# Attention added into x by accumulating transfers, h's low products apart, x's maximum one step ahead

## The reference, cut to what matters

```python
# x: 64 x 128 x 256 (batch, sequence, model); ctx the same shape
q, k, v = (LN(x) @ Wq + bq), (ctx @ Wq + bq), (ctx @ Wq + bq)      # 16 columns
corr = mean over batch and columns of circular correlation(q, k)    # 128 values
w, shift = softmax(top_k(corr, 12)), indices
R = sum_i w[i] * roll(v, -shift[i])          # repeated for 16 heads, reshaped
x = x + R @ Wout + bout
def q4(x):   # blocks of 16: scale = max|x| / 6, values to a grid of 8 with signs
    ...
n = layernorm(x)
h = silu(q4(n) @ q4(w_gate).T) * (q4(n) @ q4(w_up).T)               # 704 columns
x = x + q4(h) @ q4(w_down).T
```

## Time and profile before

| | |
|---|---|
| median of 3 runs | 575.65 us |
| the profiled execution | 575.05 us, span 573.2 us |
| VectorE busy | 461.9 us (81%) |
| TensorE busy | 466.7 us (81%) |
| ScalarE busy | 393.3 us (69%) |
| GpSimd busy | 282.7 us (49%) |
| DMA engines busy, first 50 us / main loop | 82% / 57% |
| main loop, one step | 12.9 us |

### The profile page before, as it was taken

One profiled execution on the slowest core, in us unless ns is written; L12 is line 12 of the kernel. 1 busy time (PEld: TensorE's weight loads), 2 busy tenths in 40 slices (PEclk: granted clock), 3 DMA queues, 4 the chain that ended last, 5 costly groups with the idle time before them and its releaser, 6 DMA issues. The chain is left out here.

```text
span 573.2 us, 10039 instructions
## 1 busy us (share of the span) xinstructions
PE 466.7 (81%) x3454; PEld 306.1 (53%) x3454; DVE 461.9 (81%) x742; ACT 393.3 (69%) x666; POOL 282.7 (49%) x365
## 2 busy tenths in 40 slices
PE   5086798704789999999899999999899999999944
PEld 5075687501345565556555555556555565556633
DVE  2899864315799999999899999999899999998760
ACT  2177865535778777788888777788888778776530
POOL 3045351035356666656556666656556666632221
PEclk9689999775989999999999999999999999999987
DMA  9956550043145556555655557645655556544533
GB/s 283 344 170 202 176 186 14 25 102 75 37 97 122 110 122 127 120 106 111 128 118 119 110 123 126 121 107 110 130 116 119 112 115 110 108 88 98 88 78 78
DMA packets 165042, 69.19 MB, mean 121 GB/s; under 512 B 129152, under 2 KB 164736, under 8 KB 164992
## 3 DMA queue, kind: packets, MB, share of 16 engines
q1 hardware_dynamic: 164416, 68.03, 52.2%
q10 hardware_dynamic: 576, 0.53, 0.3%
HBM read 27.90 MB, written 9.18 MB: 65 GB/s over the span
## 5 line engine op out<-in xcount | busy, mean ns | idle before, releaser
L694 PE MATMUL ps<-guT_hi,a_xT 128*128 128x512 f16 (+1 forms) x384 | 140.7, 366 | 55.2 <-DMA a_xT<-ctx_sb 55.2
L405 POOL TENSOR_TENSOR ctx_sb<-h_c,sl 128x704 f16<-128x704 f16 x64 | 96.1, 1523 | 115.8 <-DVE ctx_sb L909 115.8
L704 PE MATMUL ps<-dT_hi,hqT 128*128 128x256 f16 x704 | 132.2, 276 | 12.3 <-DMA hqT<-ctx_sb 12.3
L696 PE MATMUL ps<-guT_hi,a_xT 128*128 128x512 f16 (+1 forms) x384 | 140.3, 365 | 0.0
L695 PE MATMUL ps<-guT_lo,a_xT 128*128 128x512 f16 (+1 forms) x384 | 140.1, 365 | 0.0
L694 PEld LDWEIGHTS ps<-guT_hi,a_xT 128*128 128x128 f16 x384 | 37.7, 98 | 103.7 <-DMA a_xT<-ctx_sb 46.0
L457 ACT ACTIVATE h_c<-y_h 128x1408 bf16<-128x1408 bf16 (+3 forms) x40 | 49.2, 1230 | 61.9 <-DVE y_h L939 36.5
L706 PE MATMUL ps<-dT_lo,hqT 128*128 128x256 f16 x384 | 89.6, 277 | 0.0
L704 PEld LDWEIGHTS ps<-dT_hi,hqT 128*128 128x128 f16 x704 | 69.7, 99 | 25.2 <-DMA hqT<-ctx_sb 13.1
L443 POOL TENSOR_TENSOR xs<-xs,w_raw 128x512 f32<-128x512 f32 x32 | 37.8, 1180 | 79.5 <-issue 49.6
L904 DVE SCALAR_TENSOR_TENSOR hb<-ps,h_in,w_raw 128x704 f32<-128x704 f32 x64 | 60.5, 945 | 4.7 <-PE ps L696 4.6
(11 more groups left out here) (139 smaller groups left out, 868.8 us busy)
## 6 DMA issues: line engine op xcount, KB each, us to landing
w_raw<-a_scratch SPq DMA_DIRECT2D x64, 128.5 KB, 2.6
xs<-in_x_dram SPq DMA_DIRECT2D x16, 512.0 KB, 5.3
ctx_sb<-in_ctx_dram SPq DMA_DIRECT2D x16, 512.0 KB, 4.4
out_dram<-a_xT SPq DMA_DIRECT2D x64, 128.0 KB, 2.0
hqT<-ctx_sb SPq DMA_TRANSPOSE x64, 3.7
w_raw<-in_L_ffn_w_down_dram SPq DMA_DIRECT2D x1, 704.0 KB, 8.1
w_raw<-in_L_ffn_w_gate_dram SPq DMA_DIRECT2D x1, 640.0 KB, 5.9
w_raw<-in_L_ffn_w_up_dram SPq DMA_DIRECT2D x1, 640.0 KB, 7.1
```

What stands on the lines that cost most here:

```text
L405: pool.tensor_tensor(hq[:, j % 2, t, FF:2 * FF].rearrange("p (ih r) -> p ih r", ih=IH), h_c[:, :].bitcast(F16).rearrange("p (ih t r) -> p ...
L694: pe.matmul(dst, xt[:, c, :], guT[0][:, c, n0:n1], start=(c == 0), stop=False)
L696: last = pe.matmul(dst, xt[:, KC + c, :], guT[0][:, c, n0:n1], start=False, stop=(c == KC - 1))
L704: pe.matmul(dst, hqT[:, j % 4, c, :], dT_hi[:, c, :], start=(c == 0), stop=False)
```

## The change

The attention goes from HBM straight into x: GpSimd issues transfers that add what they bring to what is there. `xs` gets a 257th column for the mean, so one transfer adds both. `a_scratch` is laid out so that each of 8 rows holds all batch elements side by side, and one transfer takes two pairs (the first two take one each): 17 transfers, issued at the end of every second step, for pairs st + 6 and st + 7. Lines 443 and 444 and SP's loads go.

The statistics, normalisation and maximum of x each run one pair further ahead, with two buffers for `xn`; the loop starts at step -4. The maximum (949 in the changed file) stands behind y_x.

`low_h` handles one tile. The first stands where it stood; the second at the end of the step, behind a wait for y_x, and SP's second `turn_h` stands behind `turn_x`. `h_c` gets a second buffer. The factor on the scales moves into other constants, which makes the copy `s32` (428) superfluous.

```diff
-FIRST, END = -5, NP + 4
+FIRST, END = -4, NP + 4
+SUMS = (1, 1) + 15 * (2,)
...
-        xs = sb("xs", [P, B, D])
+        xs = sb("xs", [P, B, DA])
...
-        h_c = sb("h_c", [P, 2 * FF], U16)
+        h_c0 = sb("h_c", [P, 2 * FF], U16)
...
+        h_c = [h_c0[:, :], w_q[1][:, 0:2 * FF].bitcast(U16)]
...
@@ sync
-            def load_attn(n):
-                need(sp, s["x1_done"], n - 1)
-                if n % (NP // 4) == 0:
-                    sp.wait_ge(a_io[n // (NP // 4)], 16)
-                for t in range(2):
-                    row = (2 * n + t) * ROWS8 * DA
-                    sp.dma_start(attn[:, n % 2, t, :], bass.AP(a_dram.tensor, row, [[0, HEADS], [DA, ROWS8], [1, DA]])
-                                 ).then_inc(attn_loaded[n % 2], 16)
...
                 if pair_ok(st - 2):
                     turn_h(2 * st - 4)
-                    turn_h(2 * st - 3)
                 if pair_ok(st + 1):
                     turn_x(st + 1)
+                if pair_ok(st - 2):
+                    turn_h(2 * st - 3)
...
-                if pair_ok(st + 6) and st + 6 >= 2:
-                    load_attn(st + 6)
@@ gpsimd
+            def add_attn(k):
+                n0 = sum(SUMS[:k])
+                if n0 % (NP // 4) == 0:
+                    pool.wait_ge(a_io[n0 // (NP // 4)], 16)
+                row, cols = 2 * n0 * DA, 2 * SUMS[k] * DA
+                pool.dma_start(xs[:, 2 * n0:2 * (n0 + SUMS[k]), :].rearrange("p t n -> p (t n)"),
+                               bass.AP(a_dram.tensor, row, [[0, HEADS], [B * DA, ROWS8], [1, cols]]), accum_op=ALU.add
+                               ).then_inc(s[f"x1_in{k}"], 16)
...
                 if pair_ok(st - 2):
-                    low_h(st - 2)
-                n = st + 3
+                    low_h(st - 2, 0)
+                n = st + 4
...
-                    pool.tensor_scalar(s32[:, n0:n1], bm[:, 1, n0:n1], X_SCALE * DOWN, 1.0, ALU.mult, ALU.mult).then_inc(s["s32"], 1)
-                    pool.wait_ge(s["s32"], m + 1)
...
-                n = st + 4
-                if pair_ok(n):
-                    pool.wait_ge(attn_loaded[n % 2], 32 * (n // 2 + 1))
-                    need(pool, s["x4_steps"], K_XQ * (n - 2) + 1)
-                    need(pool, s["pool_st"], K_R * (n - 1))
-                    x1 = xs[:, 2 * n:2 * n + 2, :]
-                    pool.tensor_tensor(x1, x1, attn[:, n % 2, :, 0:D], ALU.add)
-                    pool.tensor_tensor(s_nm[:, n % 2], neg_mean[:, 2 * n:2 * n + 2], attn[:, n % 2, :, D], ALU.add
-                                       ).then_inc(s["x1_done"], 1)
+                if pair_ok(st - 2):
+                    if pair_ok(st + 2):
+                        pool.wait_ge(s["x4_steps"], K_XQ * (st + 2) + 1)
+                    low_h(st - 2, 1)
+                if st + 6 >= 2 and st + 6 < NP and st % 2 == 0:
+                    add_attn(st // 2 + 4)
@@ scalar
-                    act.wait_ge(s["x1_done"], b + 1)
+                    act.wait_ge(s[f"x1_in{sum_of(b)}"], 16)
...
-                    need(act, s["loh"], 2 * j)
-                    split(h_t[:, :], h_c[:, :], y_h[:, :], s["h_split"], 3 * j)
+                    need(act, s["loh"], 2 * (j - 1))
+                    split(h_t[:, :], h_c[j % 2], y_h[:, :], s["h_split"], 3 * j, X_SCALE)
@@ vector
-                if pair_ok(xb):
-                    dve.wait_ge(s["xn_ready"], xb + 1)
-                    dve.tensor_reduce(bm[:, 0, RUN_H:NS], xn.rearrange("p (b i) -> p b i", i=BLK), AX.X, ALU.max,
-                                      apply_absolute_value=True).then_inc(s["x_max"], 1)
...
+                if pair_ok(st + 3):
+                    dve.wait_ge(s["xn_ready"], st + 4)
+                    dve.tensor_reduce(bm[:, 0, RUN_H:NS], xn[:, (st + 3) % 2, :].rearrange("p (b i) -> p b i", i=BLK), AX.X, ALU.max,
+                                      apply_absolute_value=True).then_inc(s["x_max"], 1)
```

More of the change, by code:

```diff
@@ L157, in build @@
         bm = sb("bm", [P, 3, NS])
-        s32 = sb("s32", [P, NS])
         sh = sb("sh", [P, 2, 2 * NS], BF16)
@@ L220, in runs_of, with sum_of @@
             return w[:, FF * (g % 2):FF * (g % 2) + n].rearrange("p (ih c r) -> p c ih r", ih=IH, r=r)
+        def sum_of(n):
+            return next(k for k in range(len(SUMS)) if n < sum(SUMS[:k + 1]))
         def pair_ok(n):
@@ L468, in w_split @@
                     act.wait_ge(s["root_set"], 1)
-                split(h_t[:, 0:n], h_c[:, 0:n], y_h[:, 0:n], s["w_split"], 3 * g)
+                split(h_t[:, 0:n], h_c[0][:, 0:n], y_h[:, 0:n], s["w_split"], 3 * g, 1.0)
             def evac_x(i, u):
@@ L706, in down @@
                         pe.matmul(dst, hqT[:, j % 4, c, :], dT_lo[:, c, :], start=False, stop=False)
-                pe.matmul(dst, ident_out[:, :], xs[:, j, :], start=False, stop=True).then_inc(s["d_done"], 1)
+                pe.matmul(dst, ident_out[:, :], xs[:, j, 0:D], start=False, stop=True).then_inc(s["d_done"], 1)
             pe.wait_ge(s["t_steps"], 17)
```

93 lines of the change are left out of this document (44 added, 49 removed).

## The result

| | before | after |
|---|---|---|
| median (4 runs each) | 576.3 us | 696.82 us (693.7 to 699.94) |
| ratio, 95% interval | | 1.208 (1.201 to 1.214) |
| the profiled execution | 575.05 us | 699.94 us, span 698.0 |
| mean granted TensorE clock | 0.952 | 0.858 |

557 was forecast. The changed kernel is 21% slower. First its page: two lines of the chain, the two groups of instructions with the largest new idle time (it stands behind the bar), and two DMA issues, the last number being the median from issue to landing.

A forecast was written before the change was run, and what follows sets the result against it. VectorE from line 730 through y_h, then ScalarE's three passes, was taken as the closed loop. Gains of 16.8 (x maximum), 1.1 (drain) and 0.8 (startup) made 18.7 us off 575.05, so 557 us as median, range 551 to 569.

The forecast's parts named there:

- the main term: VectorE's loop step: moving the x maximum behind y_x shortens it by 0.575 us to 12.34, 16.8 us in all.
- the drain: Last three steps: line 932 takes 0.28 rather than 0.64 us once the second low product moves away, 1.1 us gained.
- the statistics: GpSimd's pow starts 0.3 us ahead of line 932: no cost taken, upper bound 11.2 us if 932 waits for it.
- the low scale: GpSimd's sl starts right after sh, beside y_h: y_h longer by 0.10 us, upper bound 0.24 or 3.9 us less gain.
- where the low product falls: Second low product of h runs 4.0 to 5.5 us after y_h's start, before line 730 at 5.79: no cost.
- the landing: Accumulating transfer lands in 2.6 to 10.6 us, hidden in the loop; h's second transposition lands 3.7 after issue, costing nothing.
- the start: Startup, before the loop: squares start 1.37 us earlier, less 0.6, net gain 0.8 us; bounds 3.1 gained to 4.9 lost.
- rival 3: Accumulating transfer delays h's second transposition by d; 15 steps lose d - 1.9 each, 584 us at d = 3.7; chance 0.08.

The follow-up runs named there:

- the late transfer: Changed kernel with GpSimd issuing the accumulating transfer some 3 us later, behind VectorE's product of h in the next step: 564.35 us (0.979).
- the first kernel with loads: Changed kernel with SP loading one pair a step and GpSimd adding it behind the second low product, instead of accumulating transfers: 586.35 us (1.016).

## Why the prediction was wrong

**Right: what bounds the kernel, and the main term.** VectorE's first part and ScalarE's passes close the loop. Forecast 12.34 us a step, measured 12.42 in the undisturbed steps of the changed kernel and in nearly all of the kernel without transfers. The idle time before h's offset: 0.3 forecast, 0.43. The term was 16.8 us; the 27 steps that took 348.70 us before take 335.76 without transfers and 334.80 with the late transfer, 12.9 and 13.9 less. It is a little large: y_h is longer by 0.18 where 0.10 was reckoned.

**Wrong by 1.1 us: the drain.** The scale takes 0.25 us there rather than 0.64, as said, but nothing is gained: the last three steps take 37.39 us before and 37.33 without transfers (511.25 to 548.64; 492.77 to 530.10).

**Right: the statistics; nearly so: the low scale.** y_h takes 1.80 us (1.72 forecast), which is the 0.08 of the step; the scale instruction stays 0.28 although pow, at 417.93, runs for 0.69 beside its start at 418.19:

```profile
417.93 0.69 POOL L418 TENSOR_TENSOR s_r<-s_ve,neg_half 128x2 f32<-128x2 f32 x1
418.70 0.19 POOL L420 TENSOR_TENSOR s_nmr<-xs,s_r 128x2 f32<-128x2 f32 x1
419.13 0.64 POOL L430 TENSOR_TENSOR sl<-bm,sh 128x240 f16<-128x240 f32 x1 [0.23 <-issue]
...
423.51 1.52 POOL L400 TENSOR_TENSOR ctx_sb<-h_c,sl 128x704 f16<-128x704 f16 x1 [3.75 <-DVE w_raw L943]
```

The section "Who interferes with whom" of the Trainium skill's page "SBUF — State Buffer" would have put the scale behind all of pow; this row doesn't bear it out for an instruction of 2 elements. The sum of 514 elements in the first kernel with loads does agree with it: the offset beside it was held by 0.83 us.

**Right: where the low product falls.** 4.07 us behind y_h's start (419.44 to 423.51), ending before the offset at 425.32. The transposition is issued 5.6 us behind y_h's start, as forecast (5.55).

**Wrong: the landing.** The step that failed reads: "so both ends are hidden in the loop", with a landing between 2.6 and 10.6 us, and behind it the second transposition, "lands 3.7 later", "Cost nothing; it is the thinnest cover in the change". The transfer landed in 14.5 us, outside both ends, and took the transposition with it: 15.25. The transfer's own result was still in time; what the forecast had put at nothing, the second transposition of h beside it, is what the 139 us are. For the forecast I had asked only when the transfer's result is needed, about 15 us later, and not what its company does to the one transfer with 0.9 us of slack. That stood under rival 3: mechanism, place and wait (line 704's idle time with the transposition as its releaser) came as written there, and got a chance of 0.08. Its size was off: d was taken from the transposition's own length (3.7, so 584 us); it is 11.5. Of the slack of 1.9 us in the price per step, d - 1.9, only the first part was left (11.55 us late, 10.62 waited: 0.93, as forecast); the other 1.0 was used up by TensorE's product, which ran at half clock behind 10.6 us of idleness and took 2.4 longer. So a long step is 11.7 us longer than a short one (24.15 against 12.42), where d - 1.9 would be 9.65. The number of such steps is 12, not 15: the first transfers are issued before h has anything to transpose. From the distances of the scale instruction, the 12 long steps take 284.4 us, 135 more than 12 of 12.42. With the kernel without transfers (558.2) that makes 693, and 696.8 was measured.

**Wrong by some microseconds, in part not the change's: the start.** 0.8 us was to be gained. The first scale instruction of the loop starts at 128.01 us, against 126.55 before and 121.08 in the kernel without transfers. The squares' first row follows the issue by 4.56 us (4.92 forecast), but the whole start is later: the correlation ended 4 us later (its last product read by ScalarE at 100.89 against 96.84 before), while TensorE's granted clock between 50 and 75 us, far ahead of every changed instruction of the loop, is lower. The windows of that stretch after, the third number from the end being the clock (1.00 before):

```profile
50.00:75.00 25.00, 18.37 (x241) 15.99 (x242) 19.64 (x59) 18.55 (x36) 9.77 (x15) 0.86 0.52 165
```

This clock doesn't go with the transfers. The kernel with the maximum put back has none and shows the same (0.86, correlation ended at 100.95); those with a pair at a time and with the transfers kept apart have them and show 1.00 (97.14 and 97.52), as does the one without transfers (96.69). Rows of 257 elements, which all of these have, have no part in it either. What makes the clock differ stays open. At a clock of 1.00 and with single pairs the loop's first scale stands at 126.18, 0.4 us ahead of before, and the first of the 27 steps at 161.60 against 162.55: the gain forecast for the start is about right there. With two pairs in a transfer it isn't: apart, also at 1.00, the first scale starts at 126.88 and the second 6.28 later (5.42 with single pairs).

The late transfer's 564.35 against 558.16 is the start: its loop has nearly the same steps (12.38 on average), its first scale instruction stands at 128.11, and the first of the 27 steps at 166.07 against 157.01 and, before, 162.55. This kernel is the change at its best so far: 12.7 us gained of the 18.7 forecast. That the kernel without transfers gains just 18.7 (576.88 to 558.16) is luck: 5.5 us of it are its start, which waits for no transfer into x.

**Open.** What makes 15 us out of a meeting that takes 7 to 8 in a kernel of its own. Shown are its conditions in the loop: this place, the accumulating kind (beside a plain copy the transposition takes 6 to 8), the size (beside half of it, 8 to 10). In the loop the queue behind and the stores are excluded. The offset of the source, the destination rows, and GpSimd's or VectorE's work each by itself are excluded only for a transfer issued 0.4 to 0.6 us behind a transposition. The loop's order, the transfer 0.09 us ahead of the transposition and none ahead of it, was never tried in a kernel of its own; it is the first thing to try, since in the loop 2.5 us ahead is nearly harmless. Not tried either is all engines at work at once beside the pair alone.

## What to carry to other kernels

When a change puts a transfer beside another, ask first what the neighbour has to lose: the slack of each transfer issued near it, not of the new one alone. Here 0.9 us of slack stood against a neighbour of 5 us and more. A median landing hid twelve long ones of 64; the wait of the consumer, with its count, shows them. And shift such a transfer by a few microseconds before giving it up: the same instruction cost 139 us at one place and some 6 at the next.

## What the runs showed of the hardware

- An accumulating transfer of 514 KB from HBM into SBUF takes 5.3 us alone, a plain one of the same shape 4.4; 257 KB accumulating take 4.0.
- Issued 0.2 to 0.4 us behind a DMA transposition (alone 3.6), in a kernel of its own, it takes 6.9 and the transposition 5.7. Issued 0.09 us ahead of one in this loop: 13.4 to 15.2 and 14.2 to 15.5; with nothing of SP's behind them the DMA engines are nearly idle for the last 4 us. Issued 2.5 us ahead of one, in the same loop: 5.7 to 7.2 and 4.6 to 6.1.
- A plain copy costs by its queue and place together: from GpSimd 0.09 us ahead of a transposition 576 us, from SP 1.4 us behind it 563, for the same bytes.
- TensorE after 10.6 us of idleness got clock 0.50 for a product of 4.70 us (2.3 at full clock).
- VectorE's scale instruction took its usual 0.28 us when it started inside a GpSimd pow of 128x2; its offset of 0.89 us took 1.72 when it started inside a GpSimd sum of 128x514.
